# Nucleus search: four evaluations in step 0, a third pair of ScalarE sums in step 1

## The chip, the cores and the metric

The kernel runs on one core of a Trainium2 chip. The metric is device time of one execution in microseconds (us); lower is better. Engines: PE is TensorE, PEld its weight loads, DVE is VectorE, ACT is ScalarE, POOL is GpSimd, SP is SyncE. L1931 is line 1931 of the kernel before.

## The reference

Four graph layers on 2048 nodes of 256 features, each with a layernorm and relu ahead and a residual: an attention layer with 8 heads, a diffusion layer, and two normalised graph convolutions. The change is in the diffusion layer, which runs two steps:

```python
for s in range(STEPS):                      # 2
    A = _adj_from_feats(Xa, W1, W2, W3)     # 2048 x 2048
    Xf = Rf @ Xf
    Xb = Rb @ Xb
    Xa = A @ Xa
    Z = Z + (Xf @ U1[s] + Xb @ U2[s] + Xa @ U3[s])
```

`_adj_from_feats` makes logits `Q @ W2 @ K.T`, sorts each row, keeps the largest values until their softmax reaches 0.9 (the nucleus, with the value that crosses it), and takes the softmax of those kept. Equal values are kept in the order of their index.

## The kernel before

The function `nucleus` (from L1429) does one step; it is called twice, with `step` 0 and 1, and phases are set apart by a barrier of all engines. The 2048 rows are 16 tiles of 128 rows, in G = 4 groups of 4 tiles. Values of two groups at a time lie in `e[:, g % 2]`. For tile k of group g:

- TensorE makes the logits into PSUM (`logits`, L1593, L[1] for group 0 and 1 alternating with L[0], later L[0] alone, so that tile after tile must be emptied first), VectorE takes the row maximum (`peak`, L1928), ScalarE the exponential with its row sum (`exp`, L1789).
- VectorE searches the threshold for the four tiles of a group together. `begin` sets the bounds; an evaluation (`cut`, C = CUTS[step] of them: 5 in step 0, 7 in step 1) is four passes `mass` (L1931: the sum of the values above `thr`), one for each tile, and `update` (L1978 to L1999), a chain of small instructions that interpolates the next threshold, from FIRST_AT, AIM and CLIP. The last update stops after the bounds.
- In step 1 the first two evaluations of groups 1 to 3 are done by ScalarE instead (`sums`, L1803: a Relu and a Sign over each of the four tiles, each with a row sum); VectorE gives it the threshold (`aim`) and takes the sums (`update_from_sums`). ScalarE waits for `aimed`, VectorE for `summed`.
- `look` (L2049, L2051) takes the eight largest values that are not above the upper bound; if the crossing is among them the row is settled. If not, `retry` bisects (L1931 again, on `nuc_small`), looks and settles until it is. In step 0 GpSimd tells whether any row is open (`ask_any`, `resolve`), then `mask` (L2154) cuts the values, and `exceeds` and `release` treat equal values. In step 1 `look` also settles (four passes of L1931 on `nuc_small`) and counts equal values, and `keep` (L2106, L2116) cuts tile by tile.
- TensorE turns the cut tile, ScalarE makes an f16 half of it (`halves`), TensorE the other's remainder, and 48 matmuls multiply with Xa (`multiply`, `product`).

Between these, TensorE and ScalarE diffuse the 16 row tiles of Xf and Xb through the transposed adjacency, which SyncE loads in two parts of 512 KB for each tile as soon as TensorE has used the one before (`diffuse`; ScalarE's part is `results`: `rows_of` scales the sums, `turned_rows`, `weighted_rows`). A diffused tile of step 1 has two products, forward and backward. In step 0 VectorE makes the f16 remainder of each diffused tile (`rest_parts`, L2015), and ScalarE may not write tile t before the remainder of tile t - 4. DIFFUSED says after which tiles each group's products stand: 10, 13, 16 in step 0, and 5, 9, 13 in step 1; BESIDE how the first ones are spread over the logits of group 1. `after` makes pieces of the next step's logits operands (step 0) or the last weighted sum (step 1) for tiles whose product is done.

Every engine runs its instructions in the order in which the code gives them; there is no planner. VectorE's order is the list at the end of its block (L2225 on): in step 0 evaluations of group g + 1 stand between look, mask and release of group g, and the peaks of group g + 2 between them. In ScalarE's list `sums(2, 0)` stands straight behind the four products of group 0, ahead of the diffused tile 5, and `sums(2, 1)` behind that tile's scaled rows; the same with tile 9 for group 3.

Of the kernel before, what the change touches and what calls it, by code (L numbers as in the profile page):

```python
# [25 lines left out]
I32 = mybir.dt.int32  # L26
U32 = mybir.dt.uint32
ALU = mybir.AluOpType
# [22 lines left out]
G = 4  # L51
CUTS = (5, 7)
FIRST_AT, CLIP = 0.3, 0.1
L2_ROOM = 128.0
BELOW_LOW = 0.02
AIM = 3.0
# [1372 lines left out]
def nucleus(nc, sb, ps, sem, name, QT, KT, parts, out, ident, diffusion, next_logits):  # L1429
# [22 lines left out]
    with ExitStack() as c:  # L1452
# [41 lines left out]
        WEIGHTED = TP[1][:, D:2 * D]  # L1494
        DIFFUSED = ((10, 13, T), (5, 9, 13))[step]
# [6 lines left out]
        with block:  # L1502
# [13 lines left out]
            def _(pe):  # L1516
# [229 lines left out]
            def _(s):  # L1746
# [45 lines left out]
                def sums(g, n):  # L1792

                    before = 2 * G * (2 * (g - 1) + n)
                    s.wait_ge(exped, G * g + G)
                    s.wait_ge(aimed, 2 * (g - 1) + n + 1)
# [46 lines left out]
                for k in range(G):  # L1843
                    exp(0, k)
                BESIDE = ((range(0, 1), range(1, 3), range(3, 5), range(5, DIFFUSED[0])),
                          (range(0, 1), range(1, 2), range(2, 3), range(3, G)))[step]
# [25 lines left out]
                if step:  # L1872
                    sums(3, 0)
                results(range(DIFFUSED[1], DIFFUSED[1] + 1), False)
                if step:
                    sums(3, 1)
                results(range(DIFFUSED[1] + 1, DIFFUSED[2]), True)
# [35 lines left out]
            def _(v):  # L1913
# [24 lines left out]
                def begin(g, tiles):  # L1938
# [13 lines left out]
                    together(nc.vector.tensor_scalar(point[s][:, 0, ks], S[:, 0, 0, ks], 1.0 - FIRST_AT, FIRST_AT * TOP_BITS, ALU.mult, ALU.add),  # L1952
                             nc.vector.tensor_scalar(thr[s][:, ks].bitcast(I32), S[:, 0, 0, ks], 1.0 - FIRST_AT, FIRST_AT * TOP_BITS, ALU.mult, ALU.add))
# [8 lines left out]
                def update_from_sums(g, n):  # L1962

                    v.wait_ge(summed, 2 * G * (2 * (g - 1) + n + 1))
# [423 lines left out]
```

## Time and profile before

| | us |
|---|---|
| median of 3 runs | 3493.71 (3493.33 to 3495.12) |
| the profiled execution's own time | 3495.69 |
| its span | 3493.5 |
| TensorE busy | 2908.3 (83%) |
| VectorE busy | 2271.2 (65%) |
| ScalarE busy | 1294.3 (37%) |
| mean granted TensorE clock | 0.929 |

The span goes from the first to the last instruction; the execution's own time holds 2.2 us more around it. Busy shares are means over phases with different limits. Step 0 of the nucleus lies at about 2014 to 2519 us of the span, step 1 at 2534 to 3242.

### The profile page before, as it was taken

To read this page: it belongs to the slowest core of one execution; us is meant where nothing else is said; L and a number is where in the kernel's file an instruction comes from. 1 tells how busy PE (TensorE), PEld (TensorE's weight loads), DVE (VectorE), ACT (ScalarE), POOL (GpSimd) and SP (SyncE) were. 2 spreads that over 40 slices of the span, in tenths; PEclk is the share of its full clock that TensorE was granted. 3 is DMA by queue.
4 is the path that set the end of the run, shared out by engine and by line. 5 is a ranking of instruction groups with operands and counts; after the bars stand their busy time and mean duration, and the time that the engine had idled before them with its cause. 6 is when DMAs were issued, how large, how long until landed. Compare 5 with 4: busy or idle time off the path is not lost. (4 is left out here: it accounts for less than half of the span.)

```text
span 3493.5 us, 57725 instructions
## 1 busy us (share of the span) xinstructions
PE 2908.3 (83%) x20376; PEld 2136.6 (61%) x20376; DVE 2271.2 (65%) x4455; ACT 1294.3 (37%) x1686; POOL 59.0 (2%) x68
## 2 busy tenths in 40 slices
PE   2469999999999999999999686867765668687599
PEld 1356676766667666676666455646544456576488
DVE  7956555555555565555656578888688987895430
ACT  4733434434344443443433322423314243432311
POOL 0000000000000000000000000000000000000110
PEclk7579999999999999999999888989887889899899
DMA  7937748477484774747748322100011010100500
GB/s 262 374 139 174 186 105 198 111 177 183 107 202 105 186 174 115 196 104 186 178 113 211 90 67 72 37 1 25 1 49 37 1 37 13 37 25 13 223 1 25
DMA packets 587852, 396.75 MB, mean 114 GB/s; under 512 B 538563, under 2 KB 553414, under 8 KB 562118
## 3 DMA queue, kind: packets, MB, share of 16 engines
q1 hardware_dynamic: 585990, 382.49, 40.5%
q10 hardware_dynamic: 1728, 12.58, 1.1%
q8 instruction: 71, 1.16, 0.1%
q14 instruction: 63, 0.52, 0.1%
HBM read 223.05 MB, written 37.75 MB: 75 GB/s over the span
## 5 line engine op out<-in xcount | busy, mean ns | idle before, releaser
L734 DVE SCALAR_TENSOR_TENSOR e_lo<-e,e_hi 128x2048 f16<-128x2048 f32 x128 | 293.3, 2291 | 441.6 <-ACT e_hi L656 441.6
L596 PE MATMUL av<-vw_hi,pT_hi 128*128 128x256 f16 x2048 | 559.5, 273 | 7.9 <-DMA pT_lo<-e_lo 7.9
L596 PE MATMUL av<-vw_lo,pT_hi 128*128 128x256 f16 x2048 | 559.5, 273 | 0.0
L596 PE MATMUL av<-vw_hi,pT_lo 128*128 128x256 f16 x2048 | 559.4, 273 | 0.0
L585 PE MATMUL logits<-kT_hi,qT_hi 128*128 128x512 f16 x1024 | 389.0, 380 | 9.2 <-DVE att_small L720 7.3
L1931 DVE SCALAR_TENSOR_TENSOR nuc_junk<-nuc_e,nuc_thr 128x2048 bf16<-128x2048 f32 x168 | 388.4, 2348 | 5.0 <-issue 0.4
L585 PE MATMUL logits<-kT_lo,qT_hi 128*128 128x512 f16 x1024 | 388.1, 379 | 0.0
L585 PE MATMUL logits<-kT_hi,qT_lo 128*128 128x512 f16 x1024 | 388.1, 379 | 0.0
L650 ACT ACTIVATE att_small<-att_small,minus 128x1 f32<-128x1 f32 x128 | 37.7, 295 | 835.5 <-DVE att_small L729 835.5
L720 DVE CUSTOM_DVE_ANT_0 e<-logits,bias,att_small 128x1024 f32<-128x1024 f32 x256 | 328.6, 1284 | 0.9 <-issue 0.3
L651 ACT ACTIVATE e<-e,att_small,sc 128x2048 f32<-128x2048 f32 x128 | 266.2, 2080 | 0.0
L656 ACT ACTIVATE e_hi<-e 128x2048 f16<-128x2048 f32 x128 | 244.5, 1910 | 15.3
L596 PEld LDWEIGHTS av<-vw_hi,pT_hi 128*128 128x128 f16 x2048 | 200.7, 98 | 44.8 <-issue 8.4
L596 PEld LDWEIGHTS av<-vw_lo,pT_hi 128*128 128x128 f16 x2048 | 200.8, 98 | 36.3
L596 PEld LDWEIGHTS av<-vw_hi,pT_lo 128*128 128x128 f16 x2048 | 200.8, 98 | 23.7
L1593 PE MATMUL nuc_l<-logit_k,logit_q 128*128 128x512 f32 x256 | 134.0, 675 | 70.4 <-ACT nuc_e L1789 63.1
L585 PEld LDWEIGHTS logits<-kT_hi,qT_hi 128*128 (+1 forms) x1024 | 99.9, 98 | 145.9 <-issue 39.0
L585 PEld LDWEIGHTS logits<-kT_hi,qT_lo 128*128 (+1 forms) x1024 | 100.2, 98 | 120.9
L1569 PE MATMUL nuc_l<-nuc_u,nuc_xsT 128*128 128x256 f32 x320 | 87.3, 426 | 100.1 <-ACT nuc_xsT L1767 94.8
L585 PEld LDWEIGHTS logits<-kT_lo,qT_hi 128*128 (+1 forms) x1024 | 100.2, 98 | 105.9
L353 PE MATMUL adj_tp<-ident,adj_rows 128*128 128x128 f32 x256 | 60.2, 414 | 95.7 <-DVE adjT L407 61.6
L1593 PEld LDWEIGHTS nuc_l<-logit_k,logit_q 128*128 128x128 f32 x256 | 53.5, 217 | 139.1 <-ACT nuc_e L1789 71.6
(400 smaller groups left out, 5764.7 us busy)
## 6 DMA issues: line engine op xcount, KB each, us to landing
bias<-bias_scratch SPq DMA_DIRECT2D x130, 1024.0 KB, 4.8
bias_scratch<-adj_bias SPq DMA_DIRECT2D x16, 1024.0 KB, 7.9
adjT_scratch<-adjT SPq DMA_DIRECT2D x16, 1024.0 KB, 8.1
nuc_at_hi<-adjT_scratch SPq DMA_DIRECT2D x32, 512.0 KB, 3.8
nuc_at_lo<-adjT_scratch SPq DMA_DIRECT2D x32, 512.0 KB, 4.5
adjT<-adjT_scratch SPq DMA_DIRECT2D x16, 1024.0 KB, 20.8
adj_rows<-in_adj_dram ACTq DMA_DIRECT2D x12, 1024.0 KB, 9.4
adj_rows<-in_adj_dram SPq DMA_DIRECT2D x4, 1024.0 KB, 7.9
```

Of the source, the lines that this page charges most:

```text
L353: last = nc.tensor.transpose(TP[q][:, t * P:(t + 1) * P], rows_u[:, t // 2, t % 2 * P:(t % 2 + 1) * P], ident[:, :])
L585: last = nc.tensor.matmul(o, QT[w][:, k, ds(t * P, P)], KT[x][:, k, c0:c0 + BANK], start=(k == 0 and w == x == 0), stop=(k == 1 and w == 1))
L596: last = nc.tensor.matmul(AV[par][:, :], PT[par][w][:, m, :], VW[x][:, m, :], start=(m == 0 and w == x == 0), stop=(m == T - 1 and w == 1))
L650: nc.scalar.activation(masked(par), nb(par), ACT.Exp, bias=minus[:, 0:1], scale=1.0)
L651: nc.scalar.activation(E[par][:, :], E[par][:, :], ACT.Exp, bias=nb(par), scale=sc[:, 0:1], accum_out=ssum(par)).then_inc(exped, 1)
L656: nc.scalar.activation(EH[:, :], E[par][:, :], ACT.Copy, scale=P_SCALE).then_inc(hi_s, 1)
L720: return nc.vector.tensor_tensor_reduce(E[par][:, cols], L[half][:, :], B[par][:, cols], 1.0, (small[:, par, 6:7], m0(par))[half], ALU.add ...
L734: nc.vector.scalar_tensor_tensor(out=EL[:, :], in0=E[par][:, :], scalar=P_SCALE, in1=EH[:, :], op0=ALU.mult, op1=ALU.subtract).then_inc(lo ...
L1569: nc.tensor.matmul(WEIGHTED, xT[:, n * D + k * P:n * D + (k + 1) * P], U[:, n, k, :], start=(n == k == 0), stop=False)
L1593: last = nc.tensor.matmul(scores_in(i)[:, b * BANK:(b + 1) * BANK], QT[:, i * P:(i + 1) * P], KT[:, b * BANK:(b + 1) * BANK], start=True, ...
L1931: nc.vector.scalar_tensor_tensor(out=void[:, k % 2, :], in0=e[:, g % 2, k, 0:N], scalar=bound[:, k:k + 1], in1=e[:, g % 2, k, 0:N], op0=co ...
```

## The change

CUTS becomes (4, 7). The starting point, the clips and the aims of the interpolation become values for each step and evaluation; those of step 1 stay at 0.3, 0.1 and 3.0. In step 0 the remainders of diffused tiles stand later in VectorE's list, the first diffused tiles are spread 1, 1, 1, 7, and the answer of GpSimd leads to a retry of each open tile instead of the whole group. `look_tiles` takes several pieces of work to put between its tiles. In step 1 there are three sums (`BY_SUMS`) for groups 1 to 3; each stands behind one diffused tile on ScalarE in groups 2 and 3, the peaks of group 1 are earlier, and `begin` and `aim` of the next group stand inside the last evaluation.

```diff
@@ -49,11 +49,12 @@
-CUTS = (5, 7)
-FIRST_AT, CLIP = 0.3, 0.1
+CUTS = (4, 7)
+FIRST_AT = (0.475, 0.3)
+CLIP = ((0.01, 0.01, 0.2), (0.1,) * 6)
...
-AIM = 3.0
+AIM = ((3.0, 4.0, 2.0, 0.0), (3.0,) * 7)
...
+        BY_SUMS = (1, 3)[step]
@@ in the blocks of TensorE and of ScalarE (there: range(3, G if step else DIFFUSED[0])) @@
-                BESIDE = ((range(0, 1), range(1, 3), range(3, 5), range(5, DIFFUSED[0])),
-                          (range(0, 1), range(1, 2), range(2, 3), range(3, DIFFUSED[0])))[step]
+                BESIDE = (range(0, 1), range(1, 2), range(2, 3), range(3, DIFFUSED[0]))
@@ -1852,16 +1852,19 @@
                     results(range(G, G + 1), True)
                     sums(1, 1)
                 last_result(DIFFUSED[0] - 1)
+                if step:
+                    sums(1, 2)
                 for k in range(G):
                     halves(0, k)
                     exp(2, k)
                     product(0, k)
                 if step:
-                    sums(2, 0)
-                results(range(DIFFUSED[0], DIFFUSED[0] + 1), False)
-                if step:
-                    sums(2, 1)
-                results(range(DIFFUSED[0] + 1, DIFFUSED[1]), True)
+                    for n in range(BY_SUMS):
+                        results(range(DIFFUSED[0] + n, DIFFUSED[0] + n + 1), n > 0)
+                        sums(2, n)
+                    results(range(DIFFUSED[0] + BY_SUMS, DIFFUSED[1]), True)
+                else:
+                    results(range(DIFFUSED[0], DIFFUSED[1]), False)
                 last_result(DIFFUSED[1] - 1)
...
@@ -2042,10 +2046,10 @@
-                def look_tiles(g, ks, behind=None):
+                def look_tiles(g, ks, behind={}):
                     for k in range(ks.start, ks.stop):
-                        if k == 1 and behind is not None:
-                            behind()
+                        if k in behind:
+                            behind[k]()
@@ -2142,12 +2146,11 @@
                 def resolve(g, n):
 
                     answered(n)
-                    load(0)
+                    load(G)
                     with v.If(v.snap(left) > 0):
-                        settle(g, ALL)
-                        any_row(z_, 0)
-                        load(0)
-                        retry(g, ALL)
+                        for k in range(G):
+                            load(k)
+                            retry(g, slice(k, k + 1))
@@ -2239,57 +2243,54 @@
                     rest_parts(0)
                     cut(0, 2)
                     peak(1, 2)
-                    rest_parts(1, 2)
+                    rest_parts(1)
                     cut(0, 3)
                     peak(1, 3)
-                    rest_parts(3, 4)
-                    cut(0, 4)
-                    rest_parts(5, 6)
+                    rest_parts(2, 3)
                     look(0)
-                    rest_parts(7, 8)
+                    rest_parts(4, 5)
                     begin(1, range(G))
                     cut(1, 0)
+                    rest_parts(6, 7)
                     resolve(0, 1)
                     mask(0, ALL)
                     exceeds(0, ALL)
-                    rest_parts(9)
+                    rest_parts(8)
                     cut(1, 1)
                     release(0, 2, ALL)
+                    rest_parts(9)
                     cut(1, 2)
                     peak(2, 0)
                     cut(1, 3)
                     peak(2, 1)
-                    cut(1, 4)
-                    peak(2, 2)
-                    look(1, lambda: peak(2, 3))
-                    rest_parts(10, 11)
+                    look(1, {1: lambda: peak(2, 2), 3: lambda: peak(2, 3)})
                     begin(2, range(G))
                     cut(2, 0)
-                    rest_parts(12)
+                    rest_parts(10)
                     resolve(1, 3)
                     mask(1, ALL)
+                    rest_parts(11)
                     exceeds(1, ALL)
                     cut(2, 1)
+                    rest_parts(12)
                     release(1, 4, ALL)
...
@@ -2303,22 +2304,25 @@
+                    def next_sums(g, n):
+                        update_from_sums(g, n)
+                        aim(g)
+
                     cut(0, 1)
                     peak(1, 0)
                     cut(0, 2)
+                    peak(1, 1)
                     cut(0, 3)
-                    peak(1, 1)
+                    peak(1, 2)
                     cut(0, 4)
-                    peak(1, 2)
+                    peak(1, 3)
                     cut(0, 5)
-                    peak(1, 3)
+                    start_sums(1)
                     cut(0, 6)
-                    look(0, lambda: start_sums(1))
-                    update_from_sums(1, 0)
-                    aim(1)
+                    look(0, {1: lambda: next_sums(1, 0)})
+                    next_sums(1, 1)
                     keep(0, 1)
-                    update_from_sums(1, 1)
-                    cut(1, 2)
+                    update_from_sums(1, 2)
                     peak(2, 0)
                     cut(1, 3)
                     peak(2, 1)
@@ -2326,13 +2330,14 @@
                     peak(2, 2)
                     cut(1, 5)
                     peak(2, 3)
-                    cut(1, 6)
-                    look(1, lambda: start_sums(2))
-                    update_from_sums(2, 0)
-                    aim(2)
+                    masses(1, range(0, 2))
+                    start_sums(2)
+                    masses(1, range(2, 4))
+                    update(1, 6)
+                    look(1, {2: lambda: next_sums(2, 0)})
+                    next_sums(2, 1)
                     keep(1, 2)
-                    update_from_sums(2, 1)
-                    cut(2, 2)
+                    update_from_sums(2, 2)
                     peak(3, 0)
```

The parts left out repeat this for group 3 in both lists, pass `[step]` and `[step][n]` to the constants, and count the blocks of sums with BY_SUMS where 2 stood.

## Rows read from the trace of the kernel before

**Rows 1.** Stretches: busy time and count of each engine, granted clock, DMA share, GB/s.

```profile
2014.00:2519.00 505.00, 380.19 (x2500) 289.17 (x2500) 406.95 (x754) 157.68 (x280) 17.43 (x18) 0.90 0.11 35
...
2534.00:3242.00 708.00, 506.00 (x3440) 398.89 (x3440) 574.21 (x1179) 244.62 (x368) 2.30 (x8) 0.88 0.08 26
...
2567.00:2749.00 182.00, 104.86 (x695) 82.85 (x692) 158.89 (x330) 54.90 (x73) 0.58 (x2) 0.80 0.09 30
```

**Rows 2.** Groups of VectorE instructions: line, operation, shapes, count, busy us, mean ns, idle.

```profile
L1931 DVE SCALAR_TENSOR_TENSOR nuc_junk<-nuc_e,nuc_thr 128x2048 bf16<-128x2048 f32 x168 | 388.4, 2348 | 5.0 <-issue 0.4
...
L2049 DVE SCALAR_TENSOR_TENSOR nuc_junk<-nuc_e,nuc_hi 128x2048 f32<-128x2048 f32 x32 | 75.2, 2350 | 2.1
...
L2051 DVE MAX8 nuc_top<-nuc_junk 128x8 f32<-128x2048 f32 x32 | 73.4, 2295 | 2.4
```

**Rows 3.** Timeline of VectorE, one evaluation and a peak: start, us, line, operation.

```profile
2180.92 2.35 DVE L1931 SCALAR_TENSOR_TENSOR nuc_junk<-nuc_e,nuc_thr 128x2048 bf16<-128x2048 f32 x1
...
2192.77 2.29 DVE L1928 TENSOR_REDUCE nuc_nmax<-nuc_l 128x1 f32<-128x2048 f32 x1
...
2194.98 2.34 DVE L1931 SCALAR_TENSOR_TENSOR nuc_junk<-nuc_e,nuc_thr 128x2048 bf16<-128x2048 f32 x1
```

**Rows 4.** Timeline of VectorE, last evaluation of a group.

```profile
2442.13 2.35 DVE L1931 SCALAR_TENSOR_TENSOR nuc_junk<-nuc_e,nuc_thr 128x2048 bf16<-128x2048 f32 x1
...
2452.90 2.35 DVE L2049 SCALAR_TENSOR_TENSOR nuc_junk<-nuc_e,nuc_hi 128x2048 f32<-128x2048 f32 x1
```

**Rows 5.** Groups of VectorE between 2040 and 2520: peaks, and remainders.

```profile
L1928 DVE TENSOR_REDUCE nuc_nmax<-nuc_l 128x1 f32<-128x2048 f32 x12 | 27.5, 2292 | 22.5 <-PE nuc_l L1593 21.9
...
L2015 DVE SCALAR_TENSOR_TENSOR xf_lo<-nuc_xs,xf_hi 128x256 f16<-128x256 f32 x16 | 6.7, 421 | 16.1 <-ACT xb_hi L1760 15.9
```

**Rows 6.** Timeline of ScalarE: exp (2,0) and exp (2,3) of step 0.

```profile
2195.10 1.97 ACT L1789 ACTIVATE nuc_e<-nuc_l,nuc_nmax 128x2048 f32<-128x2048 f32 x1 [3.88 <-DVE nuc_nmax L1928]
...
2242.19 1.96 ACT L1789 ACTIVATE nuc_e<-nuc_l,nuc_nmax 128x2048 f32<-128x2048 f32 x1
```

**Rows 7.** Timeline of TensorE at the end of step 0, idle time in brackets.

```profile
2364.51 0.27 PE L1526 MATMUL nuc_l<-x_hi,nuc_at_hi 128*128 128x256 f16 x1 [0.72 <-ACT acc L1819]
...
2418.11 1.12 PE L1608 MATMUL nuc_l<-ident,nuc_e 128*128 128x128 f32 x4 [5.21 <-DVE nuc_small L2177]
...
2487.32 3.04 PE L1685 MATMUL nuc_l<-ident,nuc_e 128*128 128x128 f32 x13 [12.46 <-DVE nuc_small L2177]
```

**Rows 8.** Timeline of VectorE, step 1: update from sums, aim, head of keep.

```profile
2694.55 0.87 DVE L2100 TENSOR_SCALAR nuc_listed<-nuc_eight,nuc_small 128x8 f32<-128x8 f32 x4 [5.91 <-issue]
...
2839.04 0.16 DVE L1965 SCALAR_TENSOR_TENSOR nuc_signs<-nuc_signs,nuc_half_t 128x4 f32<-128x4 f32 x1
...
2841.94 0.17 DVE L1958 TENSOR_SCALAR nuc_minus_t<-nuc_thr 128x4 f32<-128x4 f32 x1
```

**Rows 9.** Timeline of ScalarE: first and last of a block of sums.

```profile
2810.07 2.00 ACT L1803 ACTIVATE nuc_pThi<-nuc_e,nuc_minus_t 128x2048 f16<-128x2048 f32 x1 [9.15 <-DVEq L1923]
...
2825.88 0.19 ACT L1803 ACTIVATION_READ_ACCUMULATOR nuc_pTlo<-nuc_e,nuc_minus_t 128x1 f32 x1
```

**Rows 10.** Timeline of TensorE: first and last matmul of diffusion tile 5.

```profile
2801.06 0.27 PE L1526 MATMUL nuc_l<-xf_hi,nuc_at_hi 128*128 128x256 f16 x1 [0.72 <-ACT acc L1819]
...
2811.87 0.27 PE L1539 MATMUL nuc_l<-xb_lo,ident 128*128 128x256 f16 x1
```

**Rows 11.** Timeline of VectorE: two peaks of step 1 and their waits.

```profile
2636.96 2.29 DVE L1928 TENSOR_REDUCE nuc_nmax<-nuc_l 128x1 f32<-128x2048 f32 x1 [3.46 <-PE nuc_l L1593]
...
2914.13 2.29 DVE L1928 TENSOR_REDUCE nuc_nmax<-nuc_l 128x1 f32<-128x2048 f32 x1 [11.04 <-PE nuc_l L1593]
```

**Rows 12.** Timeline of VectorE: first of the last remainders, next phase's first instruction.

```profile
3199.42 2.48 DVE L2209 SCALAR_TENSOR_TENSOR nuc_pTlo<-nuc_l,nuc_pThi 128x512 f16<-128x512 f32 x4
...
3241.22 0.17 DVE L1039 MEMSET l_ones<- 1x128 f32 x1 [13.64 <-PEq L125]
```

More of the change, by code:

```diff
@@ L1792, in sums @@
                 def sums(g, n):
-                    before = 2 * G * (2 * (g - 1) + n)
+                    before = 2 * G * (BY_SUMS * (g - 1) + n)
                     s.wait_ge(exped, G * g + G)
-                    s.wait_ge(aimed, 2 * (g - 1) + n + 1)
+                    s.wait_ge(aimed, BY_SUMS * (g - 1) + n + 1)
                     for k in range(G):
@@ L1844, in _ @@
                     exp(0, k)
-                BESIDE = ((range(0, 1), range(1, 3), range(3, 5), range(5, DIFFUSED[0])),
-                          (range(0, 1), range(1, 2), range(2, 3), range(3, G)))[step]
+                BESIDE = (range(0, 1), range(1, 2), range(2, 3), range(3, G if step else DIFFUSED[0]))
                 for k in range(G):
@@ L1872, in _ @@
                 if step:
[L1873 to L1877, printed above, removed]
+                    for n in range(BY_SUMS):
+                        results(range(DIFFUSED[1] + n, DIFFUSED[1] + n + 1), n > 0)
+                        sums(3, n)
+                    results(range(DIFFUSED[1] + BY_SUMS, DIFFUSED[2]), True)
+                else:
+                    results(range(DIFFUSED[1], DIFFUSED[2]), False)
                 last_result(DIFFUSED[2] - 1)
@@ L1951, in begin @@
                              nc.vector.tensor_scalar(S[:, 0, 1, ks], frac[:, ks].bitcast(I32), -1.0, None, ALU.mult))
-                    together(nc.vector.tensor_scalar(point[s][:, 0, ks], S[:, 0, 0, ks], 1.0 - FIRST_AT, FIRST_AT * TOP_BITS, ALU.mult, ALU.add),
-                             nc.vector.tensor_scalar(thr[s][:, ks].bitcast(I32), S[:, 0, 0, ks], 1.0 - FIRST_AT, FIRST_AT * TOP_BITS, ALU.mult, ALU.add))
+                    together(nc.vector.tensor_scalar(point[s][:, 0, ks], S[:, 0, 0, ks], 1.0 - FIRST_AT[step], FIRST_AT[step] * TOP_BITS, ALU.mult, ALU.add),
+                             nc.vector.tensor_scalar(thr[s][:, ks].bitcast(I32), S[:, 0, 0, ks], 1.0 - FIRST_AT[step], FIRST_AT[step] * TOP_BITS, ALU.mult, ALU.add))
                 def aim(g):
@@ L2179, in release, with look @@
                     inverse(g, ks)
-                def look(g, behind=None):
+                def look(g, behind={}):
                     look_tiles(g, ALL, behind)
                     if step == 0:
-                        ask_any(z_)
+                        nc.vector.tensor_copy(ask[:, 0:G], z_)
+                        ask_any(z_, G)
                         return
@@ L2277, in _ @@
                     peak(3, 1)
-                    cut(2, 4)
-                    peak(3, 2)
-                    look(2, lambda: peak(3, 3))
-                    rest_parts(13, 14)
+                    look(2, {1: lambda: peak(3, 2), 3: lambda: peak(3, 3)})
                     begin(3, range(G))
                     cut(3, 0)
-                    rest_parts(15)
+                    rest_parts(13)
                     resolve(2, 5)
                     mask(2, ALL)
+                    rest_parts(14)
                     exceeds(2, ALL)
                     cut(3, 1)
+                    rest_parts(15)
                     release(2, 6, ALL)
@@ L2342, in _ @@
                     peak(3, 3)
-                    cut(2, 6)
-                    look(2, lambda: start_sums(3))
-                    update_from_sums(3, 0)
-                    aim(3)
+                    masses(2, range(0, 2))
+                    start_sums(3)
+                    masses(2, range(2, 4))
+                    update(2, 6)
+                    look(2, {2: lambda: next_sums(3, 0)})
+                    next_sums(3, 1)
                     keep(2, 3)
-                    update_from_sums(3, 1)
-                    for n in range(2, C):
+                    update_from_sums(3, 2)
+                    for n in range(3, C):
                         cut(3, n)
```

9 lines of the change are left out of this document (4 added, 5 removed).

## The prediction

> **What bounds the kernel now.** I read the windows first, to see which engine is full in the two stretches that the change touches. In the first nucleus phase (step 0, 505 us) VectorE is busy 407 us, in the second (step 1, 708 us) 574 us, more than TensorE in both [rows 1]. The groups of VectorE instructions come next: 168 passes over 2048 columns at 2.35 us each are the threshold search [rows 2]. They are 42 evaluations of four tiles, exactly the number written in the code (20 in step 0; 7 + 5 + 5 + 5 in step 1), and the look (L2049) ran 32 times, once per tile. So no row needed a retry. The timeline gives the unit of everything below: from one evaluation's first pass to the next instruction 11.85 us (four passes and some 20 small instructions in a chain), and 2.21 us for a peak behind it [rows 3]. The last evaluation of a group skips the interpolation: 10.77 us [rows 4]. The waits of VectorE show what else ends last: in step 0 it waits 21.9 us for TensorE's logits (four times before a peak: 5.72, 4.11, 5.84 and 6.20) and 15.9 us for ScalarE's halves of diffused tiles (before remainders, 7.05 and 7.46 the long ones), 37.8 us in all [rows 5]; in the rest of the phase VectorE sets the time.
>
> **Step 0, part by part.** Four evaluations go, one per group: 4 x 11.85 = 47.4 us of VectorE. The same number of remainders, masks, looks and peaks stays, and the DMAs of the diffused tiles stay as they are. The waits change as follows.
> Group 0: tiles are now diffused 1, 1, 1 and 7 instead of 1, 2, 2 and 5 beside the logits of group 1. Logits (1,2) follow the weighing of tile 0, which ends at 2071.7 as before, and take 3.6 us: 2075.3, before their peak at 2077.7. Logits (1,3) follow exp (1,2), from 2080.1, by 2.1 of it, 0.6 of copy, 2.3 of weighing and 3.6: 2088.7, before 2091.4. So 5.72 and 4.11 us go. What is late next is the remainder of tile 3: its ScalarE part stands behind exp (1,3), some 4.1 us after that exp starts, and VectorE waits about 3.5 us. The remainders of tiles 4 to 15 are then asked for later than they are ready (a tile every 8.06 us). ScalarE may not write tile t before remainder t-4; the tightest is tile 8 (ready at 2137, remainder 4 done at 2122), so the later remainders block nobody.
> Groups 1 and 2: from exp (g+1,0) to the end of exp (g+1,3), TensorE and ScalarE need 2242.19 + 1.96 - 2195.10 = 49.1 us, tile after tile [rows 6]; the next group repeats it (2314.61 to 2363.67). Over the same stretch VectorE now has only the last evaluation 10.8, a peak 2.2, the look 21.5 and two peaks inside it 4.4, together 38.9. So it waits 10.2 us in each of the two groups, spread over two peaks and the begin, where it waited 13.3 and 14.1.
> Waits after: 3.5 + 10.2 + 10.2 = 23.9, against 37.8; VectorE gains 13.9, and 0.7 us of issue gaps before masks (estimate from gaps of 0.3 to 2.5 there). At group 3's first release it is 47.4 + 13.9 + 0.7 = 62.0 us early.
> TensorE is not. Peak (3,0) comes 23.7 (two evaluations) + 9.9 (waits of 23.6 until there become 13.7) + 0.7 = 34.3 us early, and with it the chain of group 3's logits, so the diffusion of tiles 13 to 15 starts at 2364.51 - 34.3 = 2330.2. From there TensorE runs without a hole: 48.4 us to the end of the first four "after" pieces (2364.51 to 2418.11 less its 5.21 idle), 56.8 us for the products of group 2 and the next two pieces (2418.11 to 2487.32 less 12.46) [rows 7]: 2435.4. VectorE would let the last tiles start at 2487.3 - 62.0 = 2425.3. TensorE becomes the bound of the tail and takes back 10 us: the last tiles start 2487.3 - 2435.4 = 51.9 us earlier, and since VectorE is free then, their first remainder starts 1.3 us sooner behind them. **Step 0: 53 us.**
>
> **Step 1.** For groups 1 to 3 the third evaluation becomes a third pair of ScalarE sums. VectorE loses 11.85 and gets one more update from sums with its aim, 3.15 us (2839.04 to the end of 2841.94 and the next start) [rows 8]: 8.7 per group, 26.1 in all. The ScalarE block costs 16.0 us (2810.07 to 2826.07) [rows 9]. Now its place. In group 1 the three blocks run beside the look, the settle and keep of group 0: the first ends 0.5 us after VectorE asks, the others long before. The third is aimed at 2694.0 and ends at 2710.0 (in the clock of before, as if step 0 were unchanged), and the halves of group 0 stand behind it on ScalarE; their tile is released at about 2710.8, so it holds nobody.
> In groups 2 and 3 the first block now stands behind a whole diffusion tile (results of tile 5, of tile 9). From the end of exp (g,3): ScalarE's product 0.7, TensorE's tile 11.1 (2801.06 to 2812.14) [rows 10], the scaled rows 1.0, then 16.0 of sums: 28.8 us. VectorE meanwhile has begin and aim 1.5, two passes 4.7, the update 1.4, two tiles of look 9.6, together 17.2, and then asks. It waits 11.5 us, in each of the two groups, where it waited for no sums before. Besides it waits for exp (g,3) before begin: 2.8 and 1.2. The second and third blocks end before they are asked for (the third runs beside keep, 45 us).
> Peaks: in group 1 the earlier ones meet the logits, 1.1 + 3.9 us, where before one waited 3.46 [rows 11]. The wait of 11.04 before peak (3,0) goes, since only one diffusion tile is left behind the last sums: logits (3,0) end 6.6 us before they are wanted. Three waits of 1.16 for group 3's logits go too.
> Waits before 3.46 + 11.04 + 3.5 = 18.0, after 1.1 + 3.9 + 0.5 + 2.8 + 1.2 + 2 x 11.5 = 32.5. Net 26.1 + 18.0 - 32.5 = 11.6, **step 1: 12 us**. The tail from the first last remainder to the phase's end, 41.8 us, is unchanged [rows 12].
>
> A page bears on the waits that TensorE gets behind the sums. The row shows the granted clock at 0.80 between 2567 and 2749, where it waits twice for them [rows 1]. The Trainium skill, "TensorE: Matmul & The Clock Gate", section "Why this matters for your kernels", says that idle gaps between bursts of matmuls bring the engine back to half clock. The trace agrees there. By that rule the tile ahead of the first sums could run at 1.2 GHz, 11 us longer in each group, and the result would be 3451. I don't take it: before it stand the products of the group without a gap, and the same tile took 11.08 us there.
>
> **Sum.** 53 + 12 = 65 us. The profiled execution took 3495.7 us (span 3493.5 and 2.2 around it), 2.0 over the median: 3495.7 - 65 - 2.0 = 3428.7.
>
> **What the trace can't show** is whether four evaluations settle every row of step 0 for this data. Nothing of the spacing of the values stands in it. Below, the cost is 0; above, a retry is a bisecting pass, a look and a settling pass on one tile, 2.35 + 4.65 + 2.35 of passes and some 30 chained small instructions with a register load and branch, 16 us; a group that enters the branch also loads four flags, which took 5.9 us at the head of keep [rows 8]. I take zero, the nearest count (none in 32 looks), and keep the other end. Step 1 evaluates as often as before, at the same places up to rounding.
>
> **Rivals.**
> 1. A few retries: one or two groups of step 0 have one tile to redo, 22 us each: 3451 to 3473. For it: that five evaluations left no row open (32 looks for 32 tiles) doesn't say that four do. Against: the starting point, clips and aims are other ones, whose effect the profile can't tell, and a look takes eight values, so the search need only come near. Chance 0.14.
> 2. Slower: each of the four groups of step 0 has tiles to redo. Four groups at 22 us are 88, less the 10 us by which VectorE is ahead of TensorE at the end: 3429 + 78 = 3507. It decides from the third group with a retry, or the fourth round in all (65 us). Chance 0.14, with all that goes beyond.
> 3. The stall in the look doesn't come, because the sums or the tile before them overlap more than I read: 2 x 11.5 less, 3406. Against it is the order of ScalarE, which is strict. Chance 0.05.
> 4. The first sums are later still (the clock case above, or the DMA of the tile), 3451: 0.04.
> 5. The evaluations were hidden, no change: VectorE's waits are 38 us of 505, so this can't hold for more than a part. 0.03.
> The forecast has 0.60. The range goes from rival 3 to the end of rival 1 with some play: 3404 to 3480; the likeliest case alone is 3420 to 3437. A difference under 0.2% (7 us) can't be told from none. Faster 0.83, same 0.03, slower 0.14.
>
> **What would show it.** The passes over nuc_thr at 140 (64 in step 0, 76 in step 1) and the looks still 32; more looks, or passes over nuc_small above 16, mean retries. In step 0 TensorE without idle before the last tiles' first transposes, and VectorE idle some 10 us more at its end. In step 1 two idle times of some 11 us on VectorE inside the look, ended by ScalarE's sums. Wrong if step 0 shrinks by less than 45 us or step 1 by less than 5 or more than 20.

## The result, and the profile after

The changed kernel took 3442.05 us (median of 4 runs, 3432.39 to 3443.83), the kernel before 3494.41 us (4 runs, 3493.33 to 3495.49): ratio 0.9845, 95% interval 0.9826 to 0.9863. That is 1.55% faster. It lies inside the predicted range and 13 us above the predicted 3429, and so above the 3420 to 3437 of the likeliest case alone. Timed again beside the experiments it took 3433.02 (5 runs, 3430.66 to 3442.99), ratio 0.9829 [0.9816, 0.9843]. That median lies inside 3420 to 3437. The kernel's own spread, 13 us, is wider than that of the kernel before; what the traces say on it stands below. The profiled execution took 3443.83 us (span 3442.0).

The stretches first, as in [rows 1]: step 0, step 1, and the part of step 1 in which the clock was low before (columns: busy time and count of TensorE, its weight loads, VectorE, ScalarE and GpSimd, granted clock, DMA share, GB/s).

```profile
2014.00:2492.00 478.00, 392.76 (x2519) 293.22 (x2520) 373.80 (x703) 163.10 (x298) 17.04 (x18) 0.93 0.11 37
2492.00:3186.00 694.00, 509.78 (x3440) 401.01 (x3440) 547.31 (x1163) 291.94 (x416) 2.31 (x8) 0.89 0.08 27
2527.00:2707.00 180.00, 104.85 (x677) 81.84 (x675) 154.46 (x325) 73.44 (x92) 0.59 (x2) 0.79 0.09 30
```

The steps are measured from VectorE's first memset of one phase to that of the next (0.3 us behind its first instruction of the step). That gives for before and after: start of step 0 at 2015.5 and 2014.2 us of the span; step 0 up to the start of step 1 519.5 and 478.0; step 1 706.2 and 693.8; the rest 252.3 and 256.0. So step 0 gave 41.5 us (predicted 53), step 1 gave 12.4 (predicted 12), the start 1.3, and the rest took 3.7 back.

The groups of the threshold search, against [rows 2]:

```profile
L1935 DVE SCALAR_TENSOR_TENSOR nuc_junk<-nuc_e,nuc_thr 128x2048 bf16<-128x2048 f32 x140 | 323.7, 2348 | 6.1 <-issue 2.3
...
L2053 DVE SCALAR_TENSOR_TENSOR nuc_junk<-nuc_e,nuc_hi 128x2048 f32<-128x2048 f32 x32 | 75.2, 2350 | 2.0
...
L1935 DVE SCALAR_TENSOR_TENSOR nuc_junk<-nuc_e,nuc_small 128x2048 bf16<-128x2048 f32 x16 | 37.0, 2349 | 0.6
```

There are 140 passes, 32 looks and 16 passes over the small tile: no row was left open by four evaluations, and no retry ran.

The waits of VectorE in step 0, between 2040 and 2480, answer to [rows 5]; the first group here, the masks, was no part of those rows (idle time before the group, and what ended it, at the end of each line).

```profile
L2157 DVE SCALAR_TENSOR_TENSOR nuc_e<-nuc_e,nuc_small 128x2048 f32<-128x2048 f32 x16 | 36.7, 2348 | 12.7 <-issue 12.7
...
L1932 DVE TENSOR_REDUCE nuc_nmax<-nuc_l 128x1 f32<-128x2048 f32 x12 | 27.5, 2292 | 18.8 <-PE nuc_l L1595 18.2
...
L2019 DVE SCALAR_TENSOR_TENSOR xf_lo<-nuc_xs,xf_hi 128x256 f16<-128x256 f32 x16 | 6.7, 421 | 4.0 <-ACT xb_hi L1761 3.5
```

Peaks 18.2 and remainders 3.5 make 21.7, and two waits of 1.50 and 1.84 before `begin` bring it to 25.0; forecast 23.9. The new thing is 12.7 us of "issue" before the masks. The same group of the kernel before, over 2040 to 2520:

```profile
L2154 DVE SCALAR_TENSOR_TENSOR nuc_e<-nuc_e,nuc_small 128x2048 f32<-128x2048 f32 x16 | 36.9, 2349 | 5.8 <-issue 4.1 <-POOL nuc_flag L1907 1.7
```

In step 1 the two stalls inside the look are there, on the timeline of VectorE (start, duration, line, operation, idle time before it and what ended it):

```profile
2780.23 0.17 DVE L1969 SCALAR_TENSOR_TENSOR nuc_signs<-nuc_signs,nuc_half_t 128x4 f32<-128x4 f32 x1 [11.14 <-ACT nuc_pTlo L1804]
...
2940.26 0.17 DVE L1969 SCALAR_TENSOR_TENSOR nuc_signs<-nuc_signs,nuc_half_t 128x4 f32<-128x4 f32 x1 [11.48 <-ACT nuc_pTlo L1804]
```

The peaks of [rows 11] now wait 0.76 and 4.05 us, and peak (3,0) not at all:

```profile
2566.35 2.29 DVE L1932 TENSOR_REDUCE nuc_nmax<-nuc_l 128x1 f32<-128x2048 f32 x1 [0.76 <-PE nuc_l L1595]
...
2584.38 2.29 DVE L1932 TENSOR_REDUCE nuc_nmax<-nuc_l 128x1 f32<-128x2048 f32 x1 [4.05 <-PE nuc_l L1595]
...
2859.99 2.29 DVE L1932 TENSOR_REDUCE nuc_nmax<-nuc_l 128x1 f32<-128x2048 f32 x1
```

The tail of TensorE in step 0 answers to [rows 7] (idle time before in brackets):

```profile
2334.59 0.27 PE L1528 MATMUL nuc_l<-x_hi,nuc_at_hi 128*128 128x256 f16 x1 [0.71 <-ACT acc L1820]
...
2376.24 3.44 PE L1672 MATMUL nuc_l<-nuc_xsT,w 128*64 128x256 f32 x8 [0.69 <-ACT nuc_xsT L1829]
...
2389.12 0.69 PE L1610 MATMUL nuc_l<-ident,nuc_e 128*128 128x128 f32 x4 [0.52 <-issue]
...
2446.08 2.05 PE L1687 MATMUL nuc_l<-ident,nuc_e 128*128 128x128 f32 x16
```

The last tiles (L1687) have no idle time before them, where there were 12.46 us: TensorE is the bound of the tail, as forecast. VectorE's first release of group 3 comes at 2434.10, 12 us before they start:

```profile
2434.10 0.06 DVE L2180 MEMSET nuc_small<- 128x2 f32 x1 [1.08 <-issue]
```

### The profile page after: what moved, and what is told of

It reads as the page before. It is cut to its first block and busy times, and to the rows that moved or that the text cites. A ratio compares the mean times of both kernels' runs of the same rounds, so it can differ in the third digit from the quotient of the medians.

```text
span 3442.0 us, 57642 instructions
## 1 busy us (share of the span) xinstructions
PE 2917.1 (85%) x20376; PEld 2140.5 (62%) x20376; DVE 2201.1 (64%) x4355; ACT 1340.9 (39%) x1734; POOL 58.7 (2%) x68
## 5 line engine op out<-in xcount | busy, mean ns | idle before, releaser
L1935 DVE SCALAR_TENSOR_TENSOR nuc_junk<-nuc_e,nuc_thr 128x2048 bf16<-128x2048 f32 x140 | 323.7, 2348 | 6.1 <-issue 2.3
```

The source lines that it names most:

```text
L1935: nc.vector.scalar_tensor_tensor(out=void[:, k % 2, :], in0=e[:, g % 2, k, 0:N], scalar=bound[:, k:k + 1], in1=e[:, g % 2, k, 0:N], op0=co ...
```

## The experiments

Times from the start of a step are from VectorE's first memset in it. "Release" is the first release of group 3 in step 0, "last turn" is TensorE's first transpose of the last tiles. In the kernel before they come 471.7 and 471.8 us after the start, in the profile after 419.9 and 431.9. All ratios are to runs of the kernel before on the same chip, which had medians of 3493.41 to 3494.76 us. The four kernels with the sums first, with the old points and with four passes more ran on a second chip, where the kernel after has no run; differences in us between them and the kernel after go across chips.

**The kernel after, again**

> The changed kernel once more, unaltered, for the spread: its four executions lay between 3432 and 3444 us, the kernel before between 3493 and 3496. My theory: the spread is TensorE's granted clock in the parts where TensorE is the bound (end of step 0, the phases after), so a median near 3442 with single executions down to 3432. Rival: the spread is VectorE's issue gaps, then executions of one kernel differ in those gaps and not in the clock.

3433.02 us; in its profile step 0 takes 474.2, step 1 696.0, the rest 254.3; release 418.4, last turn 428.1. The five runs were 3430.66, 3432.20, 3433.02, 3440.48 and 3442.99. Two profiles of one kernel differ by 3.8 us in the last turn and by 1.5 in the release. VectorE's idle time before the masks is 12.6 us here and 12.7 there, so the rival finds nothing at that place. TensorE's mean granted clock over the whole execution was 0.937, 0.936 and 0.936 in the three runs up to 3433.02, and 0.935 in the two above 3440. That goes with the theory, though a mean doesn't say where the clock was lost.

**Each step alone**

```diff
 one kernel: step 0 of after, lists and BY_SUMS of before in step 1
-        BY_SUMS = (1, 3)[step]
+        BY_SUMS = (1, 2)[step]
 the other: step 1 of after; CUTS, points, BESIDE, retry and list of before in step 0
-CUTS = (4, 7)
+CUTS = (5, 7)
```

> Step 0 as changed, step 1 as before (two sums, its old order). Additive theory: the changed kernel without the 12 us of step 1, so 3454 us (40 us under before). Rival, that step 1 gained from where step 0 left the clock or the DMAs: 3445 or less.

> Step 0 as before (five evaluations, old constants, old order and old retry), step 1 as changed. Additive theory: 12 us under before, 3482 us, with both waits of some 11 us for ScalarE's sums inside the look. Rival: the two waits eat the whole gain, 3494.

Step 0 alone: 3452.04 us (4 runs), ratio 0.9874 [0.9859, 0.9889]; step 1 alone: 3484.84 (8 runs), ratio 0.9974 [0.9964, 0.9985]. Gains of 42.7 and 9.9 us, together 52.6; both in one kernel gave 52.4 in the first comparison and 61.7 in the one beside these runs. So the gains add only to within 9 us, which the spread of 13 us doesn't tell from nothing. In the profile of step 0 alone, step 1 takes 710.2 us, 4.0 longer than in the kernel before, whose lists it has there; this wasn't followed.

**The old retry in step 0**

```diff
-                    load(G)
+                    load(0)
                     with v.If(v.snap(left) > 0):
-                        for k in range(G):
-                            load(k)
-                            retry(g, slice(k, k + 1))
+                        settle(g, ALL)
+                        any_row(z_, 0)
+                        load(0)
+                        retry(g, ALL)
...
-                        nc.vector.tensor_copy(ask[:, 0:G], z_)
-                        ask_any(z_, G)
+                        ask_any(z_)
```

> Only the retry of step 0 undone: one retry for the whole group again, with one flag, its code a fourth as long. No row needs it, so only the branch over it differs. My theory: the issue gaps before the four masks (2.44, 3.78, 2.52, 3.99 us) come from the branch over the longer code; they fall to 0.3 to 2.5 as before, 6 us less in sum, 3437 us. Rival: the gaps come from where the remainders now stand or from fetching instructions at that place anyway; then they stay, and 3442.

3435.03 us (5 runs, 3434.18 to 3438.91), ratio 0.9832 [0.9818, 0.9845], not to be told from the kernel after. But its trace is another one. The body of the branch never ran in either kernel, and still the masks' idle time falls from 12.7 to 2.7 us:

```profile
L2158 DVE SCALAR_TENSOR_TENSOR nuc_e<-nuc_e,nuc_small 128x2048 f32<-128x2048 f32 x16 | 36.7, 2347 | 2.7 <-POOL nuc_flag L1911 1.7 <-issue 1.0
```

The releases of groups 0 to 3 come at 145.0, 248.2, 351.5 and 409.1 us, where the kernel after again had them at 147.3, 252.2, 358.3 and 418.4: 2.3, 4.0, 6.8 and 9.3 us earlier. The last turn comes at 423.0, only 5.1 earlier, since TensorE bounds the tail.

**What in the branch costs it: a shorter and a longer body**

```diff
 short: one loop over the group as above, flags still asked tile by tile
 long: the body of after twice
                         for k in range(G):
                             load(k)
                             retry(g, slice(k, k + 1))
+                        for k in range(G):
+                            load(k)
+                            retry(g, slice(k, k + 1))
```

> The kernel after, with the flags asked tile by tile as there (one more copy of four columns, and its flag of the group), but the skipped branch in step 0 holds the one loop of the kernel before (the whole group) in place of four loops of one tile. My theory: VectorE's idle time of 2.5 to 4 us before the masks is the jump over the long branch, so it falls to some 0.3 to 1.4 us as in the run with the group's retry, and the first release of group 3 comes about 409 to 411 us after the step's start (418 with the long branch). The rival: it is the loading of the flag from another column or the additional copy, then the idle times and the 418 stay.

> The kernel after, with the branch in step 0 twice as long: eight skipped loops of one tile in place of four. If the idle time before the masks grows with the length of what is skipped, it is 5 to 8 us in place of 2.5 to 4 and group 3's first release comes at 425 to 430 us; if it is a fixed price for a jump beyond some distance, it stays at 2.5 to 4 and the release at 418 to 420. I lean to the second (0.65).

Short body: 3431.69 us (4 runs), ratio 0.9826 [0.9811, 0.9841]; release 409.2, last turn 424.7. Long body: 3433.17 (4 runs), ratio 0.9827 [0.9812, 0.9842]; release 419.1, last turn 426.1. The masks of the short and then of the long one:

```profile
L2158 DVE SCALAR_TENSOR_TENSOR nuc_e<-nuc_e,nuc_small 128x2048 f32<-128x2048 f32 x16 | 36.7, 2349 | 2.5 <-issue 2.5
```

```profile
L2160 DVE SCALAR_TENSOR_TENSOR nuc_e<-nuc_e,nuc_small 128x2048 f32<-128x2048 f32 x16 | 36.8, 2349 | 13.0 <-issue 13.0
```

So it is what stands in the body that is jumped over, not the added copy or the other flag. The sums are 12.1 to 13.6 us over the four jumps in the seven profiles with four loops and no retry (2.1 to 4.3 at one jump), 13.0 with eight loops (2.5 to 4.0), and 2.5 and 2.7 with one loop (0.0 to 1.7), so the price didn't grow from four loops to eight. One loop isn't always that cheap: in the kernel before, with the same one-loop body, the four idle times are 1.35, 2.52, 0.26 and 1.72, in sum 5.8, so the place of the jump plays a part as well. In neither kernel did the time of the whole move beyond the spread. The Trainium skill, "Runtime: NRT & Kernel Launch", section "Instruction fetch mechanics", says that a taken branch whose target lies beyond the pages that have been fetched must first have its page fetched. The steps of the idle time (12.7 with four loops, 13.0 with eight, 2.5 with one) agree with that rule; no run here shows the fetch itself.

**The sums ahead of the diffusion tiles in step 1**

```diff
-                    for n in range(BY_SUMS):
-                        results(range(DIFFUSED[0] + n, DIFFUSED[0] + n + 1), n > 0)
-                        sums(2, n)
-                    results(range(DIFFUSED[0] + BY_SUMS, DIFFUSED[1]), True)
+                    sums(2, 0)
+                    results(range(DIFFUSED[0], DIFFUSED[0] + 2), False)
+                    sums(2, 1)
+                    results(range(DIFFUSED[0] + 2, DIFFUSED[0] + 3), True)
+                    sums(2, 2)
+                    results(range(DIFFUSED[0] + 3, DIFFUSED[1]), True)
 and the same for group 3
```

> The kernel after, with one change on ScalarE in step 1, groups 2 and 3: its list begins with the first block of sums and only then copies the halves of diffusion tiles 5 and 6 (tiles 9 and 10 in group 3), then the second block, one tile's halves, the third block, the rest. My theory: the two idle times of 11.1 and 11.5 us of VectorE inside its look come from the diffusion tile that stands ahead of the first sums, so they go, and step 1 shrinks by about 22 us if nothing else is late behind it: 3411 to 3421, where the kernel after takes 3433 to 3442. The rival: the tiles that are now copied 16 us later on ScalarE hold TensorE (its diffusion of the next tile has no free PSUM bank) and then the logits of the next group, so the wait only moves to a later peak: 3430 to 3442.

3417.83 us (5 runs, 3411.14 to 3421.72), ratio 0.9783 [0.9769, 0.9796], the interval wholly below that of the kernel after. Step 1 takes 675.6 us. The groups of updates from sums, first of the kernel after and then of this one, in step 1:

```profile
L1969 DVE SCALAR_TENSOR_TENSOR nuc_signs<-nuc_signs,nuc_half_t 128x4 f32<-128x4 f32 x9 | 1.4, 158 | 23.2 <-ACT nuc_pTlo L1804 23.2
```

```profile
L1973 DVE SCALAR_TENSOR_TENSOR nuc_signs<-nuc_signs,nuc_half_t 128x4 f32<-128x4 f32 x9 | 1.4, 157 | 2.5 <-ACT nuc_pTlo L1804 2.5
```

The 23.2 us become 2.5, and step 1 is 18.2 us shorter than in the profile after. The peaks wait 12.6 us in place of 12.0, so the wait did not move to them; a small part moved to the `begin` of group 3, which waits 4.54 us for ScalarE in place of 2.34. The theory holds: the order of ScalarE's list cost more than the third pair of sums had gained.

**The old points with four evaluations**

```diff
-FIRST_AT = (0.475, 0.3)
-CLIP = ((0.01, 0.01, 0.2), (0.1,) * 6)
-AIM = ((3.0, 4.0, 2.0, 0.0), (3.0,) * 7)
+FIRST_AT = (0.3, 0.3)
+CLIP = ((0.1,) * 3, (0.1,) * 6)
+AIM = ((3.0,) * 4, (3.0,) * 7)
```

> The kernel after, with four evaluations in step 0 still, but with the starting point (0.3), the clip (0.1) and the aim (3.0 at every evaluation) of the kernel before in place of the new ones. It tells what a retry costs, and whether four evaluations are enough by themselves. My theory from the prediction: four evaluations leave rows open if the points are not chosen for it, so at least one group retries, each tile redone at some 22 us: 3455 to 3530 with one to four groups of retries. The rival (four evaluations suffice whatever the points): the time of the kernel after, 3433 to 3442, and no pass over the small tile beyond 16.

3627.49 us (4 runs), ratio 1.0384 [1.0368, 1.0400]: slower than before by 134 us, and beyond what I expected. The count of the passes tells why:

```profile
L2053 DVE SCALAR_TENSOR_TENSOR nuc_junk<-nuc_e,nuc_hi 128x2048 f32<-128x2048 f32 x44 | 103.4, 2350 | 3.0
...
L1935 DVE SCALAR_TENSOR_TENSOR nuc_junk<-nuc_e,nuc_small 128x2048 bf16<-128x2048 f32 x40 | 93.4, 2350 | 2.9 <-issue 0.7
```

44 looks are 12 beyond the 32, and 40 small passes are 24 beyond the 16, two for each: 12 rounds of retry. The releases come at 244.6, 382.7, 522.9 and 615.9 us, against 147.3, 252.2, 358.3 and 418.4: the delays grow to 97.3, 130.5, 164.6 and 197.5, so every group retried: six rounds in group 0 and two in each of the others, by the looks of the timeline. The six retry looks of group 0 start 16.2 to 16.9 us apart, and 197.5 / 12 = 16.5 us a round, where the prediction worked out 16. The 5.9 us for each group's flags, which it put on top, don't show: by it, 12 x 16 + 4 x 5.9 would be 215.6 us, not 197.5. So rival 2's mechanism is real and its price for a round right; it was the new points, not the mere number four, that kept it away. Which of the three (start, clip, aim) does it was not tried.

**VectorE's slack, by four passes more**

```diff
 in step 0, one kernel:                        the other:
                     cut(3, 2)                                    cut(1, 2)
+                    masses(3, range(G))      +                    masses(1, range(G))
                     cut(3, 3)                                    peak(2, 0)
```

> The kernel after, with four more passes over the finished thresholds' values (one extra counting of group 3, 9.4 us of VectorE) ahead of the last evaluation of group 3 in step 0; nothing else waits for them. My theory: TensorE bounds the tail of step 0 and VectorE is some 10 to 12 us ahead there, so 0 to 2 us longer than the kernel after (3433 to 3444). The rival: VectorE still bounds the tail, and the kernel is 9.4 us longer (3442 to 3452).

> The kernel after, with the same four extra passes (9.4 us of VectorE) in group 1 of step 0, ahead of the peak of group 2. My theory: VectorE sets the time up to the peaks of group 3, less what the waits for the logits of group 2 cover: the peaks of group 2 wait 5.1 and 3.4 us just behind it for a chain that itself starts with TensorE's weighing, not with VectorE, so about 5 to 9 us are hidden there if that chain does not wait for VectorE, and none if it does; I expect 4 to 9.4 us longer than the kernel after. The rival: TensorE bounds the whole of step 0 already, 0 to 2 us longer.

In group 3: 3436.35 us (5 runs), ratio 0.9836 [0.9822, 0.9849]. The release moves from 418.4 to 427.8, by the whole 9.4, and the last turn follows it at 427.9; TensorE, which would have been free, waits:

```profile
2442.95 2.40 PE L1687 MATMUL nuc_l<-ident,nuc_e 128*128 128x128 f32 x10 [5.01 <-DVE nuc_small L2180]
```

9.4 less 5.0 are 4.4 us of slack, not the 10 to 12 that I expected, in an execution where TensorE kept its full clock through the tail (below). In the two profiles of the kernel after, where the clock fell there, the last turn comes 12.0 and 9.7 us behind the release: the slack depends on the clock. In group 1: 3444.49 us (4 runs), ratio 0.9863 [0.9848, 0.9878]; the release of group 1 is 12.2 us later (264.4 against 252.2), that of group 3 10.1. None of it is hidden, and 2.8 us come on top that weren't explained: the peaks of group 2 wait 5.54 and 3.39 us there too, since their chain starts at VectorE's own peak (2,0). The time is 11.5 us over that of the kernel after again, where I had said 4 to 9.4; VectorE sets the time of the first three groups.

**The old places of diffusion tiles 1 to 9**

```diff
-                BESIDE = (range(0, 1), range(1, 2), range(2, 3), range(3, DIFFUSED[0]))
+                BESIDE = ((range(0, 1), range(1, 3), range(3, 5), range(5, DIFFUSED[0])),
+                          (range(0, 1), range(1, 2), range(2, 3), range(3, DIFFUSED[0])))[step]
```

> The kernel after, with diffusion tiles 0 to 9 of step 0 put beside the logits of group 1 as in the kernel before (1, 2, 2, 5 in place of 1, 1, 1, 7). By the waits of my prediction: peaks (1,2) and (1,3) wait for TensorE 5.7 and 4.1 us again, and the 3.5 us before remainder 3 go, so VectorE is 6.3 us later from group 1 on: 3436 to 3448, and the release of group 1 comes 6 us later. The rival: the logits had slack anyway, no change in the releases (147, 252, 358, 418).

3448.57 us (4 runs, 3448.09 to 3450.33), ratio 0.9870 [0.9855, 0.9885]. Peaks (1,2) and (1,3) wait again:

```profile
2080.79 2.29 DVE L1934 TENSOR_REDUCE nuc_nmax<-nuc_l 128x1 f32<-128x2048 f32 x1 [5.70 <-PE nuc_l L1595]
...
2100.33 2.29 DVE L1934 TENSOR_REDUCE nuc_nmax<-nuc_l 128x1 f32<-128x2048 f32 x1 [5.93 <-PE nuc_l L1595]
```

Forecast 5.7 and 4.1. The releases come 7.5, 8.7, 9.3 and 9.5 us later, more than the 6.3 of the forecast, so the moved tiles are worth 7.5 to 9.5 us of VectorE's time by themselves. The time is 0.6 us beyond the range that I gave.

**Both gains together**

> The kernel after, with both edits that gained on VectorE: the sums ahead of the diffusion tiles in step 1, and the retry of a whole group in step 0 as the kernel before has it. My theory (the gains are of separate stretches): VectorE's releases in step 0 come some 9 us earlier, as in the run with the group's retry alone, but TensorE bounds the tail, so the last tiles start only some 4 to 5 us earlier; with the 18 to 20 us of step 1: 3409 to 3416. The rival: TensorE takes all of the 9 us back, 3416 to 3420, like the run with the sums alone.

3416.49 us (5 runs, 3413.85 to 3421.47), ratio 0.9774 [0.9761, 0.9788]. It has the lowest median, but 3416.49 lies at the border of my range and the rival's, its runs span 7.6 us, and its interval covers most of that of the sums alone: which of the two holds isn't decided. In the profile the release is at 409.0 and the last turn at 424.6, 3.5 us earlier than in the second profile of the kernel after, where the clock fell in the tail too, and 2.0 later than with the sums alone, where it didn't. This kernel also gives the sums' place by itself on the first chip: it differs from the one with the old retry (3435.03) in nothing else, and is 18.5 us faster. Its step 1 takes 680.2 us, 4.6 more than that of the other kernel with the sums first.

## Why the prediction was right, and where it was off

**No retries**, the assumption that carried the chance of 0.60: right (32 looks). The profile of before could not tell it, and the old points show how much hung on it.

**Step 1, 12 us**: 12.4 in the profile after, 10.2 in its second profile. The first sums stand behind a whole diffusion tile and VectorE waits 11.14 and 11.48 us (forecast 11.5 each), the peaks 0.76 and 4.05 (1.1 and 3.9), `begin` 2.40 and 2.34 (2.8 and 1.2), the first sums of group 1 0.54 (0.5), peak (3,0) nothing. Moving the sums ahead removed both stalls and shortened step 1 by 18.2 us, so this cause is shown. The near hit has some luck in it: VectorE's idle time ahead of the lists in `keep` (L2100 before, L2104 after) fell from 29.0 to 26.1 us, which the sum didn't hold. The low clock that was weighed for this tile (rival 4) did not come: the granted clock was 1.00 over both tiles, between 2752 and 2763 and between 2912 and 2923.

**Step 0, 53 us**: 41.5 in the profile after, 45.3 in the second profile of it; below the 45 at which I said I would be wrong in the first, just above it in the second. The count (47.4 us) and the waits were right: 25.0 for 23.9. Two terms were mis-sized.

The first is the sentence "0.7 us of issue gaps before masks (estimate from gaps of 0.3 to 2.5 there)" as a gain. The masks' idle time did not fall by 0.7 but rose by 6.9 (5.8 to 12.7). I read the edit of `resolve` as a price only where a row is open, and gave nothing for jumping over it. The release was forecast 62.0 us early; with the short body it is 62.5 early (471.7 to 409.2), with the body of the change 51.8 (419.9) and in the second profile 53.3 (418.4). The arithmetic of VectorE's chain held, the term did not.

The second is the tail of TensorE. Forecast: the diffusion of tiles 13 to 15 starts 34.3 us early, then 48.4 us to the products, then 56.8 to the last turn, 51.9 early in all. Measured in the profile after, with its first memset of step 0 at 2014.2 (2015.5 before, from which 2364.51 is 349.0): the start at 320.4 is 28.6 early, 5.7 short. Most of that is VectorE's jumps, which delay the peaks of group 3 too: with the old retry the start is at 313.9, 35.1 early, and in three profiles with the jumps (the second of the kernel after, the sums first, the passes in group 3) at 318.3 to 318.5, 3.6 to 3.8 short. The other 2 us are this execution's own: peak (3,2) waits 6.34 us for TensorE, where those three have 4.94 to 5.08. Then 54.5 us in place of 48.4, and 57.0 in place of 56.8. 5.7 + 6.1 + 0.2 = 12.0, and 51.9 - 12.0 is the measured 39.9 (471.8 to 431.9).

Of the 6.1 us, 0.5 are an idle time before the products that the sum took out, and 5.6 go with the clock: 1.8 in the diffusion of tiles 13 to 15 (the granted clock was 0.72 between 2341 and 2347) and 3.9 behind it. In the kernel with the sums first the same stretch takes 48.4 us without that idle time, the forecast to the tenth. Here is the granted clock of TensorE over the pieces behind the diffusion, in the profile after (columns: stretch, its length, TensorE's busy time and count, clock, DMA share, GB/s):

```profile
2360.00:2365.00 5.00, 3.75 (x21) 1.00 0.01 3
2365.00:2370.00 5.00, 3.28 (x15) 1.00 0.00 0
2370.00:2375.00 5.00, 3.28 (x15) 1.00 0.00 2
2375.00:2380.00 5.00, 4.00 (x12) 0.68 0.00 0
2380.00:2385.00 5.00, 3.60 (x9) 0.50 0.00 0
2385.00:2389.00 4.00, 3.13 (x8) 0.74 0.00 2
```

and in the kernel with the sums first, whose step 0 is the same program:

```profile
2355.00:2360.00 5.00, 3.75 (x21) 1.00 0.01 3
2360.00:2365.00 5.00, 3.28 (x15) 1.00 0.00 0
2365.00:2370.00 5.00, 3.28 (x15) 1.00 0.00 0
2370.00:2375.00 5.00, 3.39 (x14) 1.00 0.00 2
2375.00:2380.00 5.00, 3.46 (x14) 1.00 0.00 0
```

One and the same group of eight matmuls, the fourth of L1672 in a row of four, shows the two levels: mostly 1.2 GHz in the profile after, 2.4 GHz with the sums first.

```profile
2383.70 3.73 PE L1672 MATMUL nuc_l<-nuc_xsT,w 128*64 128x256 f32 x8 [0.69 <-ACT nuc_xsT L1829]
```

```profile
2376.43 2.14 PE L1672 MATMUL nuc_l<-nuc_xsT,w 128*64 128x256 f32 x8 [0.69 <-ACT nuc_xsT L1829]
```

In the 20 us before the fall both were engaged alike, in short bursts with idle times of 0.56, 0.69 and 0.47 us for ScalarE's copies. From the last matmul with the adjacency of tile 15 (L1528) to the first transpose of the products (L1610) it takes 29.4 us where the clock stayed at 1.00 (the runs with the sums first, with the passes in groups 1 and 3, and with the long body), and 32.4 to 34.2 in the other seven profiles with four evaluations and no retry. Three of the four ran on the second chip; the long body ran on the first, as did six of the seven (of the seventh, the profile after, the chip isn't recorded). So the chip may play a part. In the kernel before the clock fell too, but later, into its products (TensorE's row at 2418.11 of [rows 7] takes 1.12 us), behind an idle time of 5.21. With the sums first, at full clock, the last turn comes at 422.6, 49.2 us early and 2.7 from the forecast, though the jumps are in it. This is also a likely reason for the spread of the kernel's times, together with the rest (below): the executions of the kernel after that were profiled, both with the lower clock, are among its slower ones, 3443.83 and 3440.48, and its faster ones, down to 3430.66, have no profile. The long body, with the clock up behind the diffusion, took 3431.09. What decides which of the two an execution gets is open, and filling the holes was not tried.

So VectorE's lead over TensorE of 10 us at the end of step 0 came out at 12.0 and 9.7 partly by luck. The release came 10.2 and 8.7 us later than forecast, for the jumps, and the last turn 12.0 and 8.2, for the jumps and the lower clock, so that two errors of about one size leave the difference. With the sums first, at full clock, it was 3.6 us (419.0 to 422.6).

VectorE's 9.3 us of jumps also cost less than they measure: the group's retry alone took the last turn 5.1 us earlier, and the time not at all beyond the spread.

**The rest, 0 us**: 3.7 longer in the profile after (256.0), 2.0 in the second; of the other eleven profiles eight have 251.9 to 252.7, as before, and three 255.7 to 256.1. The surplus goes with the clock here too. Between 50 and 100 us behind the start of this phase the granted clock was 0.95 to 0.97 in the five profiles with more than 254 us and 1.00 in all nine others, the kernel before among them. The prediction took the rest as unchanged, which left no room for it.

**Rivals.** 1 and 2 did not come, but their price per round, 16 us, was measured at 16.5. My range of them was too mild: four groups at one round each would be 88 us; the twelve rounds cost 197.5 us of VectorE's time, and 194 us of the kernel's against the kernel after again. Rival 3 (no stall) fell in the kernel after, and is what the kernel with the sums first makes of it: 3417.83, where it named 3406. Rival 5 fell.

## What to carry to other kernels

A branch that is never entered can have a price that depends on what it jumps over: look at the idle time "issue" behind it, and keep the rare case short where VectorE sets the time. Here that was worth 9 us of VectorE's chain, and nothing of the kernel's time beyond the spread. When a search gets fewer rounds, the points have to be chosen for that number and the retries counted in the trace, as the same four rounds cost 194 us more with the old points. And when work moves to another engine, the first piece that somebody waits for goes ahead of what stands in that engine's list: here 14 to 18 us of step 1 in the profiles and 18.5 us between two kernels on one chip, more than the 12 that the move had gained.

## What the runs showed of the hardware

A jump on VectorE over a body of four loops that never ran left it idle for 2.1 to 4.3 us, over eight 2.5 to 4.0, over one 0.0 to 1.7 in the changed kernel and 0.3 to 2.5 in the kernel before. TensorE's granted clock fell from 1.00 to 0.50 in some executions and not in others of the same instructions, in bursts of 0.6 to 2.1 us with holes of 0.5 to 0.7. Between the diffusion and the products it cost 3 to 5 us where it fell, and in the phases behind the nucleus 2 to 4.
